# A three-layer decoder on one core: order of the first loads, one semaphore per weight, and the experts' constant products behind tile 0

## The reference

```python
x = _layernorm(x + attn(x, Wq, bq, Wk, bk, Wv, bv, Wo, bo))   # 16 heads of 32
x = _layernorm(x + mlstm(q=x, k=ctx, v=ctx, Wi, bi, Wf, bf, ln_scale))
x = _layernorm(x + experts(x, ...))

# attn
q = (x @ Wq.T + bq).reshape(B, S, H, D)
k = (x @ Wk.T + bk).reshape(B, S, H, D)
v = (x @ Wv.T + bv).reshape(B, S, H, D)
q = _apply_rope(q, cos, sin)
k = _apply_rope(k, cos, sin)
qk = jnp.einsum('bshd,bstd->bsht', q, k) / jnp.sqrt(jnp.float32(D))
att = jax.nn.softmax(qk, axis=-1)
out = jnp.einsum('bsht,bstd->bshd', att, v)
...
return out @ Wo.T + bo
```

## Time and profile before

| what | value |
|---|---|
| three runs, median | 2014.83 us (2012.02 to 2021.79) |
| profiled execution, its own time | 2007.69 us |
| its span | 2006.2 us |
| mean granted TensorE clock | 0.936 |
| TensorE busy | 1854.5 us (92%) |
| VectorE busy | 1551.2 us (77%) |
| ScalarE busy | 778.7 us (39%) |
| GpSimd busy | 774.0 us (39%) |
| DMA, mean over the span | 70 GB/s |

### The profile page before, as it was taken

One profiled execution on the slowest core, in us unless ns is written; L12 is line 12 of the kernel. 1 busy time (PEld: TensorE's weight loads), 2 busy tenths in 40 slices (PEclk: granted clock), 3 DMA queues, 4 the chain that ended last, 5 costly groups with the idle time before them and its releaser, 6 DMA issues.

```text
span 2006.2 us, 67466 instructions
## 1 busy us (share of the span) xinstructions
PE 1854.5 (92%) x27656; PEld 1536.5 (77%) x27656; DVE 1551.2 (77%) x3898; ACT 778.7 (39%) x2193; POOL 774.0 (39%) x779
## 2 busy tenths in 40 slices
PE   0889999999999999999999999999999999999985
PEld 0678888887887887788788878878878877887863
DVE  4456777888878788887888888777887788887776
ACT  1223344344434434443443444344344344344341
POOL 1124344344334334433433443343344344344342
PEclk9988898999989999999999999899998999999895
DMA  4111122212221221211222122212212212221110
GB/s 137 59 65 55 65 65 76 75 65 77 79 74 58 78 74 63 79 71 64 75 79 74 63 79 77 75 58 78 74 63 74 74 63 74 74 83 58 63 54 27
DMA packets 53829, 141.14 MB, mean 70 GB/s; under 512 B 8767, under 2 KB 10431, under 8 KB 45578
## 3 DMA queue, kind: packets, MB, share of 16 engines
q1 hardware_dynamic: 53770, 140.31, 20.4%
HBM read 122.98 MB, written 17.30 MB: 70 GB/s over the span
## 4 chain that ended last, share of the span: by engine, by line
PE 83%; DVE 6%; ACT 6%; issue 3%; SPq 1%; POOL 0%; DMA 0%; POOLq 0%; ACTq 0%; DVEq 0%
PE bank L477 13%; PE bank L355 13%; PE bank L356 13%; PE bank L358 12%; PE bank L347 8%; PE quad L467 4%; PE bank L434 3%; PE bank L446 3%; PE bank L491 3%; PE bank L503 3%; PE bank L448 3%; PE bank L351 2%; ACT x_high L563 2%; DVE x L931 1%; ACT gs L599 1%
## 5 line engine op out<-in xcount | busy, mean ns | idle before, releaser
L713 POOL TENSOR_TENSOR ex<-ex,w_rec 128x512 f32<-128x512 f32 x64 | 67.6, 1056 | 766.5 <-DVE w_rec L827 766.5
L621 ACT ACTIVATE Dx<-Mb,a_col 128x128 f32<-128x128 f32 x1024 | 312.8, 395 | 0.0
L725 POOL TENSOR_TENSOR h_rs<-h_ve,half_neg 128x16 f32<-128x16 f32 x64 | 201.3, 3146 | 220.9 <-DVE h_ve L913 220.9
L477 PE MATMUL bank<-c,Dx 128*128 128x33 f32 x2048 | 270.3, 295 | 16.5 <-ACT LT L651 14.5
L477 PEld LDWEIGHTS bank<-c,Dx 128*128 128x128 f32 x2048 | 262.9, 211 | 23.8 <-ACT LT L651 21.5
L594 ACT ACTIVATE x1T<-bank 128x512 f32<-128x512 f32 x64 | 38.3, 598 | 356.1 <-PE bank L347 356.1
L892 DVE SCALAR_TENSOR_TENSOR Dx<-quad,Dx 128x512 f32<-128x512 f32 x256 | 159.0, 683 | 11.4 <-PE quad L467 2.8
L739 POOL TENSOR_TENSOR rs<-ve,half_neg 128x1 f32<-128x1 f32 x192 | 106.0, 552 | 153.3 <-DVE ve L848 153.2
L718 POOL TENSOR_SCALAR_AFFINE_SELECT Dx<-Dx 128x512 f32<-128x512 f32 x256 | 160.1, 638 | 5.5 <-ACT Dx L621 5.5
L355 PE MATMUL bank<-wv_high,x_high 128*128 128x512 f32 x256 | 151.0, 590 | 0.0
L347 PE MATMUL bank<-id_sb,x 128*128 128x128 f32 x512 | 85.3, 290 | 54.9 <-DVE x2sq L933 53.0
(11 more groups left out here) (157 smaller groups left out, 4551.4 us busy)
## 6 DMA issues: line engine op xcount, KB each, us to landing
Mb<-m_rows SPq DMA_DIRECT2D x64, 1024.0 KB, 4.6
xb<-in_x SPq DMA_DIRECT2D x256, 64.0 KB
xr<-in_x SPq DMA_DIRECT2D x64, 256.0 KB, 2.6
cb<-in_ctx SPq DMA_DIRECT2D x64, 256.0 KB, 3.6
out_dram<-yo SPq DMA_DIRECT2D x64, 256.0 KB, 2.4
Dx<-in_wq SPq DMA_DIRECT2D x4, 256.0 KB, 4.7
Dx<-in_wk SPq DMA_DIRECT2D x4, 256.0 KB, 5.5
Mb<-in_wv SPq DMA_DIRECT2D x4, 256.0 KB, 6.2
```

The lines of the kernel that those rows point to most:

```text
L477: last = mm(bank[6 + h // 8][:, (h % 8) * HD:(h % 8 + 1) * HD], Dx[t.parity()][:, h % 4, h // 4, :], c1[:, h, :], start=True, stop=True)
L621: last = go(Dx[t.parity()][:, j, n, :], Mb[t.parity()][:, h, :], ACT.Exp, bias=a_col[t.parity()][:, h:h + 1], scale=-1.0)
L725: tt(h_rs[:], h_ve[:], half_neg[:], ALU.pow).then_inc(s.hrs_sb, 1)
```

## The change

Loads: tile 0 is loaded first, then the identity and the three biases (`first`, semaphore `first_in`), then the weights, each under its own semaphore (`w_in[n]`), then tile 0's ctx, the other eight constants, tile 0's residual copy, and tile 1. The scratch places of the weights are now called `staged`.

VectorE scales wq when wq alone has landed, splits q's bias and wq, makes x_low of tile 0, and then does bias and weight of k and of v. The experts' products (`products`) come at the end of VectorE's step 0, the copy of their sum (`keep_shift`) at the start of its step 2, and TensorE's matmuls for it (`shift`) at the start of its step 2. ScalarE rounds x_high of tile 0 between wq and wk. The waits for all constants move to the engines' step 1. The rest of wo gets a semaphore of its own (`low_o_set`). In the written-out steps TensorE's p_q, p_k, p_v and a_proj wait for their own weight and bias.

```diff
-        once = """const_in w_in bias_step prod_set shift_ps scale_set
-            shift_set pads_set high_set low_set center_set""".split()
+        once = """const_in first_in bias_step prod_set shift_ps scale_set ones_set
+            shift_set pads_set high_set low_set low_o_set center_set""".split()
...
             load_x(Tile(0))
-            load_res(Tile(0))
-            load_ctx(Tile(0))
+            for dst, src in first:
+                sp.dma_start(dst, src).then_inc(s.first_in, 16)
             for n, w in enumerate((wq, wk, wv, wo)):
                 for c in range(CH):
-                    sp.dma_start(w_in[n][c], w[c * P:(c + 1) * P]).then_inc(s.w_in, 16)
+                    sp.dma_start(staged[n][c], w[c * P:(c + 1) * P]).then_inc(s.w_in[n], 16)
+            load_ctx(Tile(0))
+            for dst, src in consts:
+                sp.dma_start(dst, src).then_inc(s.const_in, 16)
+            load_res(Tile(0))
             load_x(Tile(1))
...
             def p_q(t):
-                if t.k == 0 and t.regs is None:
-                    pe.wait_ge(s.low_set, 4)
+                if t.regs is None:
+                    pe.wait_ge(s.low_set, 1)
+                    pe.wait_ge(s.bias_step, 5)
+                    pe.wait_ge(s.ones_set, 1)
                 pe.wait_ge(s.xlow_sb, upto(t))
...
             def p_k(t):
+                if t.regs is None:
+                    pe.wait_ge(s.low_set, 2)
+                    pe.wait_ge(s.bias_step, 10)
...
             def p_v(t):
+                if t.regs is None:
+                    pe.wait_ge(s.low_set, 3)
+                    pe.wait_ge(s.bias_step, 15)
+                    if t.k > 0:
+                        pe.wait_ge(s.shift_set, 1)
...
-            pe.wait_ge(s.const_in, CONST_IN)
-            pe.wait_ge(s.prod_set, 3)
-            pe.wait_ge(s.pads_set, PADS)
-            for c in range(CH):
-                last = mm(bank[4][:, 0:NW], ones_f[:], wx_prod[:, c, :], start=(c == 0), stop=(c == CH - 1))
-            last.then_inc(s.shift_ps, 1)
-            pe.wait_ge(s.shift_set, 1)
-            pe.wait_ge(s.bias_step, 15)
-            pe.wait_ge(s.center_set, 11)
+            pe.wait_ge(s.first_in, FIRST_IN)
+
+            def shift():
+
+                pe.wait_ge(s.prod_set, 3)
+                pe.wait_ge(s.QT_sb, 2)
+                pe.wait_ge(s.VG_sb, 1)
+                for c in range(CH):
+                    last = mm(bank[4][:, 0:NW], ones_f[:], wx_prod[:, c, :], start=(c == 0), stop=(c == CH - 1))
+                last.then_inc(s.shift_ps, 1)
 
             def step(a):
                 b, c, d, e, f, g = [a.older(n) for n in range(1, 7)]
+                if a.regs is None and a.k == 1:
+                    pe.wait_ge(s.const_in, CONST_IN)
+                    pe.wait_ge(s.pads_set, PADS)
+                    pe.wait_ge(s.center_set, 11)
+                if a.regs is None and a.k == 2:
+                    shift()
...
-            act.wait_ge(s.const_in, CONST_IN)
-            act.wait_ge(s.w_in, 16 * 4 * CH)
-            act.wait_ge(s.scale_set, 1)
+            act.wait_ge(s.scale_set, 2)
             for n in range(4):
+                act.wait_ge(s.w_in[n], 16 * CH)
                 for c in range(CH):
-                    last = go(w_high[n][:, c, :], w_in[n][c], ACT.Copy)
+                    last = go(w_high[n][:, c, :], staged[n][c], ACT.Copy)
                 last.then_inc(s.high_set, 1)
-            act.wait_ge(s.low_set, 4)
-            act.wait_ge(s.pads_set, PADS)
+                if n == 0:
+                    p_xT(Tile(0))
...
-            pool.wait_ge(s.const_in, CONST_IN)
             nc.gpsimd.memset(half_neg[:], -0.5).then_inc(s.pads_set, 1)
             nc.gpsimd.memset(c1[:], 1.0).then_inc(s.pads_set, 1)
+            pool.wait_ge(s.const_in, CONST_IN)
...
+            dve.wait_ge(s.w_in[0], 16 * CH)
             for c in range(CH):
...
+                last = ts(staged[0][c], staged[0][c], float(D) ** -0.5, None, ALU.mult)
+            last.then_inc(s.scale_set, 1)
+            split_bias(0)
+            split_weight(0)
+            p_low(Tile(0))
+            split_bias(1)
+            split_weight(1)
+            split_bias(2)
+            split_weight(2)
```

More of the change, by code:

```diff
@@ L53 @@
 LAGS = 6
-PADS = 7
+PADS = 6
 PEEL = 10
@@ L235, in bass_decoder @@
             ve3_sb rs3_sb yo_sb""".split()
-        four = "Dx_sb Dm_sb C_sb".split()
+        four = "Dx_sb Dm_sb C_sb w_in".split()
         two = "x_in c_in r_in mb_in".split()
@@ L241, in bass_decoder @@
         s = namedtuple("Semaphores", semaphores)(**semaphores)
-        w_in = [[Dx[0][:, i].rearrange("p c n -> p (c n)") for i in range(CH)],
+        staged = [[Dx[0][:, i].rearrange("p c n -> p (c n)") for i in range(CH)],
                 [Dx[1][:, i].rearrange("p c n -> p (c n)") for i in range(CH)],
@@ L248, in bass_decoder @@
         bias_rest = [t[0:1, :] for t in (x1[0], x1[1], x2[0])]
+        first = [(id_sb[:], ident), *[(bias_in[n], bqkv[:, n * E:(n + 1) * E]) for n in range(3)]]
+        FIRST_IN = 16 * len(first)
         consts = [
-            *[(bias_in[n], bqkv[:, n * E:(n + 1) * E]) for n in range(3)], (bo_sb[:], bo.broadcast_to([P, E])), (id_sb[:], ident),
+            (bo_sb[:], bo.broadcast_to([P, E])),
             (wg_sb[:], w_gate.rearrange("(m c p) n -> p m c n", p=P, c=CH)), (bg_sb[:], b_gate),
@@ L675, in step @@
                     p_VG(b)
-                if a.real():
+                if a.real() and not (a.regs is None and a.k == 0):
                     p_xT(a)
@@ L1046, in _, with split_weight @@
[L1046 to L1049, removed]
-            nc.vector.tensor_copy(wx_shift[:], bank[4][:, 0:NW]).then_inc(s.shift_set, 1)
-            dve.wait_ge(s.shift_set, 1)
-            for n in range(3):
-                dve.wait_ge(s.high_set, n + 1)
-                for c in range(CH):
-                    last = tt(w_low[n][:, c, :], w_in[n][c], w_high[n][:, c, :], ALU.subtract)
-                last.then_inc(s.low_set, 1)
+            def split_weight(n):
+                dve.wait_ge(s.high_set, n + 1)
+                dve.wait_ge(s.w_in[n], 16 * CH)
+                for c in range(CH):
+                    last = tt(w_low[n][:, c, :], staged[n][c], w_high[n][:, c, :], ALU.subtract)
+                last.then_inc(s.low_set, 1)
@@ new lines, in _, with products @@
+            dve.wait_ge(s.w_in[0], 16 * CH)
+            for c in range(CH):
+                last = ts(staged[0][c], staged[0][c], float(D) ** -0.5, None, ALU.mult)
[7 more added lines that the diff above has]
+            split_weight(2)
+            def products():
+                dve.wait_ge(s.const_in, CONST_IN)
+                dve.wait_ge(s.pads_set, PADS)
+                for c in range(CH):
+                    middle = wx_sb[:, c, 2 * nw:NW]
+                    tt(wx_prod[:, c, 0:nw].rearrange("p (n r) -> p n r", r=NR),
+                       wx_sb[:, c, 0:nw].rearrange("p (n r) -> p n r", r=NR),
+                       middle.unsqueeze(2).broadcast_to([P, NX, NR]), ALU.mult)
+                    last = tt(wx_prod[:, c, nw:2 * nw].rearrange("p (n r) -> p n r", r=NR),
+                              wx_sb[:, c, nw:2 * nw].rearrange("p (n r) -> p n r", r=NR),
+                              debias_sb[:, c, :].unsqueeze(2).broadcast_to([P, NX, NR]), ALU.mult)
+                last.then_inc(s.prod_set, 1)
+                tt(wx_prod[:, :, 2 * nw:NW], wx_sb[:, :, 2 * nw:NW], wx_sb[:, :, 2 * nw:NW],
+                   ALU.mult).then_inc(s.prod_set, 2)
@@ L1059, in step, with keep_shift @@
+            def keep_shift():
+                dve.wait_ge(s.shift_ps, 1)
+                nc.vector.tensor_copy(wx_shift[:], bank[4][:, 0:NW]).then_inc(s.shift_set, 1)
             def step(a):
                 b, c, d, e, f, g = [a.older(n) for n in range(1, 7)]
+                if a.regs is None and a.k == 2:
+                    keep_shift()
+                if a.regs is None and a.k == 4:
+                    dve.wait_ge(s.shift_set, 1)
                 if b.real():
@@ L1110, in step @@
                     m_scan(b)
+                if a.regs is None and a.k == 0:
+                    products()
             steps(dve, step)
```

30 lines of the change are left out of this document (13 added, 17 removed).

## The result

| | before | after |
|---|---|---|
| three runs, median | 2014.83 us | 2182.81 us (2174.57 to 2190.73) |
| ratio | 1 | 1.0826 (95% interval 1.0748 to 1.0903) |
| profiled execution, its own time | 2007.69 us | 2190.73 us |
| mean granted TensorE clock | 0.936 | 0.880 |
| first neg_max | 64.65 us | 37.98 us |

I forecast 1988 us. The start came out nearly as worked out: the first neg_max is 26.7 us earlier. But the loop, in which no instruction was changed, takes 199.7 us longer, 7.68 for each pair of tiles. 199.7 + 6.0 + 4.0 - 26.7 = 183.0, the whole difference of the two spans (2189.2 - 2006.2).

What follows compares the result with a forecast made beforehand. TensorE, busy 92% of the span, was the bound, except at the start with 42.24 us of idling. 33.9 - 4.4 - 2.3 - 0.5 = 26.7, say 27, off the median 2014.83 gave 1988 us; range 1974 to 2001.

Steps and rivals of the forecast that it cites:

- Behind it the pipeline of tiles is the same in both: From VectorE's first neg_max to the end both kernels take the same time, within 7 us.
- the term for the added waits: Added TensorE waits in the ten written-out tiles cost nothing; dozens of waits cost 0.1 us in an earlier comparison.
- The clock rival: Earlier start turns loop pairs slow, 3.2 us each; all 18 give 2046 us; chance 0.08, 0.03 of it over 0.5% slower.
- wq landed: At the start, the first weight's transfer ends at 9.6 us, so TensorE starts q at 17.0.
- transfers are late: Rival: wq is delayed behind tile 0's slow pieces; wq at 14 gives gain 22.5, 1992 us; chance 0.18.
- The constants: At the start, tile 0's ctx and the other constants, loaded behind the weights, are there at 23.7 us.
- The collision: GpSimd's wo_low runs beside VectorE's wv_low from 24.3 us and stretches it, ending at 31.7 instead of 27.3: +4.4.
- QT and KT: VectorE's copies after wv_low read PSUM and stay 0.7 us long each, unaffected by GpSimd.
- the products beside the scores: VectorE's nine moved expert products, 1.3 us in all, lie beside TensorE's scores and cost nothing; uncovered, up to 6.7 us.
- The clock at v: TensorE idles from 25.5 to 33.5 us, its clock falls, and v's products run slow: +2.3 us.
- neg_max: VectorE's first neg_max starts at 35.1 us instead of 64.65, a gain of 29.5.
- The shift product in step 2: Its TensorE matmuls, moved between x1's transposes and the gate, cost +0.5 us, between 0 and 2.2.

Runs made afterwards that it cites:

- a_tile0_waits: Kernel after, its new weight, bias and shift waits only in the first tile needing them; loop starts 5 places further down than before (+5): 2011.88 us, ratio 0.9954.
- a_lean: Kernel after, new waits only in the first tile needing them, some repeated waits removed; loop starts 14 places further up than before: 1989.38 us, ratio 0.9894.
- a_shift256: Kernel after with 403 further met waits ahead of TensorE's first q; loop starts 256 places further down than before: 1990.57 us, ratio 0.9886.
- a_shift240: Kernel after with 371 further met waits ahead of q; loop starts 240 places further down than before, like -16 within a block: 1989.66 us, ratio 0.9872.
- -40: Kernel after with 323 further met waits ahead of q; loop starts 216 places further down than before, like 40 up within a block: 2224.32 us (2 runs).
- b_shift55: Kernel before with 109 further met waits ahead of TensorE's first matmul; loop starts 55 places further down, nothing else changed: 2195.50 us, ratio 1.0938.
- a_loop_pause: a_lean with 40 met waits heading TensorE's loop round, two more repeated waits removed; 1778-instruction loop starts at -22 against before: 2065.66 us (2 runs), ratio 1.0297.

## Why the prediction was wrong

**The step that failed.** "Behind it the pipeline of tiles is the same in both", and with it the term for the added waits, put at nothing: "so a few more cost nothing". Measured, the way from the first neg_max to the end is 209.7 us longer, 199.7 of it in the loop. In time they cost little: 55 instructions of 0.1 us are 5.5 us at most, spread over ten tiles; after, with them, takes 272.9 us from the first to the tenth neg_max, a_tile0_waits and a_lean, without them, 266.5 and 272.0. What I left out is that a wait also takes a place in the instruction list. I compared two stretches of the kernel before, and these cannot show what a shifted loop does. The page of before has the line of 42 code packets, and in its trace they stop once the loop has come round. That TensorE's code is fetched, and that the loop is held, could be read there; I read neither.

**The clock rival** had the right sign and too small a price: "with all 18 it is 2046", 31 us over the kernel before where 168 were measured, for it priced clock alone and at most 3.2 us a pair. I gave it 0.08 with its slower part at 0.03. Its mechanism, a new phase that deals the slow pairs anew, was wrong: a_lean and a_shift256 have the new phase and 58.80 and 58.97 us a pair. What low clock the loop has over before goes with pauses that it did not have then.

**The other terms,** predicted and measured in after:

- wq landed at 11.33 instead of 9.6, and q started at 18.9 instead of 17.0. Some of "transfers are late", 1.7 us of it.
- The constants landed at 24.72 instead of 23.7.
- The collision: 4.4 was forecast. wv_low took 5.58 instead of 2.4, and I had not counted that bias instructions beside GpSimd stretch too (1.64 instead of 0.68 in the row above; the two casts ahead of it took 0.80 and 1.40 instead of 0.42). That is 3.2 and 2.3, together 5.5.
- QT and KT as forecast; the products beside the scores cost nothing, 0.14 apiece.
- The clock at v: 2.3 forecast. v's products start 0.43 us apart at first and 0.23 from 39.97 on, so about 1.0.
- neg_max: 35.1 forecast, 37.98 measured, so a gain of 26.7 there and not 29.5: 1.7 of the 2.9 is the late wq, 1.1 the longer collision and 0.5 the longer way from KT's end to neg_max (2.45 instead of 1.99); some 0.4 came back in the other steps. Behind neg_max the lower price at v gives 1.3 back.
- The shift product in step 2: 0.5 forecast. Its matmuls took 1.09 and the 0.69 of idling ahead of the gate went, but I had left out the added wait of v of tile 1 for VectorE's copy: TensorE idled 2.10 us for it, a row shown above. Together 1.09 + 2.10 - 0.69 = 2.5.

So where the loop stays in, the forecast of the whole holds: a ratio of 0.9867 is within the intervals of a_lean, a_shift256 and a_shift240 (0.9894, 0.9886, 0.9872; medians 1989.38, 1990.57 and 1989.66, the last two with waits of their own that put the first neg_max at 40.14 and 38.61). In us their gains are 19 to 23 and not 27, as their chips' kernel before stood at 2009.97 to 2012.54; so part of the closeness of 1988 to 1989.38 is luck.

**What stays open.** How many places the window really has: -22 (with the longer loop) and -16 are in, +5 is on the edge, -40 is out, which the 35 of the arithmetic (15 for the longer loop) allow and do not prove. Whether eight blocks are held was not measured by itself: that the kept loop touches seven and the fetched one eight is worked out from its length and the fast and slow places, and no view shows blocks being kept. Why two loops that are fetched anew and have the same place differ (1703.8 and 1730.1 us) I can't say, nor why the first ten tiles and the tail differ by some us between kernels with the same loop.

## What to carry to other kernels

An instruction added anywhere ahead of a long loop moves the loop, and a wait is an instruction (or half of one); once a loop's body nears the size of what the chip holds of an engine's code, read its length in the compiled program and move it, by padding or better by taking out waits that repeat earlier ones, until the packets stop (where the edges of the blocks lie could not be told from the list here). In a profile look at the instruction queue's packets before and after, and at idle time put down to "issue" at the first instruction of the loop. And when all of an engine's instructions get slower by a few per cent at a lower clock, look for new pauses first: here 1.2 us in 59 cost 3.0.

## What the runs showed of the hardware

- A loop of 1758 TensorE instructions ran for 1500 us with no code fetched, or fetched nine packets of 16 KB in each round, by its place alone: 42 or 43 packets against 277, 1524 to 1535 us against 1704 (b_shift55) and 1730 (after).
- A wait instruction whose semaphores are long there costs about 0.1 us on TensorE (201 in 21 us, a_shift256).
- A pause of 1.2 us once in a round of 59 (a_loop_pause against a_lean) went with a granted clock of 0.93 instead of 0.96: 14 instead of 8% of the round at the low level.
- Even VectorE instructions on one partition stretch beside GpSimd: in after the cast of 1x512 at 25.63 us took 1.40 us instead of 0.42.
